# The fourth step of a sum of four, moved from GpSimd's additions to accumulating DMAs

## The chip, the cores and the metric

The kernel runs on one core of a Trainium2 chip. The metric is the device time of one execution in microseconds (us), given as the median of three runs. One further execution was profiled. Its engines are TensorE (PE in the rows; PEld are its weight loads), VectorE (DVE), ScalarE (ACT), GpSimd (POOL) and SyncE (SP, which here only issues DMAs).

## The reference

One decoder layer on x of shape (2, 2048, 512) in float32: self-attention, cross-attention and a mixture of experts, each followed by a residual sum and a layer norm. The change is in the self-attention:

```python
qkv = (x @ qkv_w + qkv_b).reshape(b, n, 3, H, D)     # H = 16, D = 32
q, k, v = jnp.moveaxis(qkv, 2, 0)
attn = jnp.einsum('bnhd,bmhd->bhnm', q, k) * scale
attn = jax.nn.softmax(attn, axis=-1)
out = jnp.einsum('bhnm,bmhd->bnhd', attn, v).reshape(b, n, c)
out = out @ proj_w + proj_b
```

The softmax's denominator is the sum over the keys of the exponentials. How that sum is formed is what is changed.

## The kernel before, in words

Self-attention takes units of four heads of one batch row (8 units), and in each unit chunks of 512 queries (4), so there are 32 chunks; the last one, `LAST`, is run apart. A chunk has 16 steps (`kt`), one for each tile of 128 keys.

In a step and for each of four heads `j`, TensorE does a maximum pass (`max_pass`, line 677, tile `sa_mx`: scores of the *next* chunk, of which VectorE takes the maximum over the keys, line 554) and a score pass (`score`, line 745, tile `sa_sc`: this chunk's scores, keys on the partitions, with the maximum already subtracted). ScalarE takes the exponential of each score bank (line 509) into `prob[:, kt % 4, j, :]`, a ring of four steps of 128x512 for each of four heads. There are three banks for maxima and two for scores, so TensorE runs at most that far ahead of VectorE and ScalarE. Every second step TensorE has a burst (`burst`): the products with the values for the two steps before (`add_values`, line 693, tile `sa_pv`), and, in steps with `kt % 4 == 2`, the row sums (`row_sums`, line 701, tile `sa_den`). Pieces of the projections of later units stand between the passes (lines 661 and 667, tile `sa_misc`); VectorE splits each finished projection in two parts (lines 546 and 548, tile `sa_hilo`), and SP moves these within SBUF to the operand stacks (line 279). SP also loads 1 MB blocks of the transposed input (line 348, tile `sa_xT`).

TensorE need not sum every step: four steps of exponentials are added elementwise first, into `quad_sum[:, d % 2]` (128 x 4 heads x 512, two buffers; `d` counts the sums, four in a chunk). The sum is made in halves of two heads (128x1024):

- `add_step(g, i, k)` on GpSimd, for k = 1, 2, 3, line 309: step k is added to the sum so far; for k = 1 the sum so far is step 0 itself. In front of it stands a wait for the exponentials of those heads, and for k > 1 a wait for the addition before.
- The second half of the first addition (k = 1, half 1) is VectorE's: `add_pair`, line 560, placed by `PAIR_AT = (2, 1)` in VectorE's order, after the second maximum of the third step of four.
- So there are five additions of GpSimd and one of VectorE for a sum (`ADDS = 5`), each announced by a semaphore: `quad_ready` for GpSimd's, `pair_ready` for VectorE's. `added(engine, d, k, half)` is the wait for one of them.

Who waits for a sum: TensorE's `row_sums(d)` for the last addition, half 1 of k = 3. It comes two steps after the sum's last step (`DEN_LAG = 6`). ScalarE, in `exponentials`, waits before it overwrites a ring place for the addition that read it: j = 0 and j = 2 of step `kt` wait for addition `max(kt % 4, 1)` of the sum before. The first addition of a sum waits for the row sums of the sum two before (`den_mm`), which read the same buffer.

The order on each engine is fixed by the program. GpSimd has the three `add_step` of each sum in turn, and once a chunk, after (i, k) = `DIVIDE_AT` = (1, 1), the division of the chunk before (line 315). VectorE has, in each step, four maxima, and at listed places the splits (`LEAVE_AT`), the pair's addition, the reciprocals (`INVERT_AT`, line 587) and the shift.

Of the kernel before, what the change touches and what calls it, by code (L numbers as in the profile page):

```python
# [9 lines left out]
ALU = mybir.AluOpType  # L10
# [57 lines left out]
def make_ident(pool, ident, zeroed, ready):  # L68

    pool.memset(ident[:, :], 0.0).then_inc(zeroed, 1)  # L70
    pool.wait_ge(zeroed, 1)
    pool.affine_select(out=ident[:, :], in_=ident[:, :], compare_op=ALU.not_equal, fill=1.0,
                       base=0, pattern=[[-1, P]], channel_multiplier=1).then_inc(ready, 1)


def self_attention(nc, z, keep, block, x, xT_dram, qkv_w, qkv_b, attnT_dram, rows_dram):


    B, N, C, KC, G, HG, D, T, NQ = z.B, z.N, z.C, z.KC, z.G, z.HG, z.D, z.T, z.NQ
# [15 lines left out]
    W, SKIP, SLOT_TILES, EMPTIES = C + 2, 2 ** 20, z.E * z.CAP // P, 2  # L95


    QUADS, ADDS = T // 4, 5
    PAIR_AT = (2, 1)
    DEN_LAG = 6  # L100


    LAST, LAST_DEN_AT = CHUNKS - 1, 11
# [60 lines left out]
    s = Stage(nc, left, "sa", keep)  # L164
# [9 lines left out]
    prob = s.sb("prob", [P, 4, HG, BANK])  # L174
    quad_sum = s.sb("quad_sum", [P, 2, HG, BANK])
# [38 lines left out]
    shift_mm, shiftT_ready, shift_in = s.sem("shift_mm"), s.sem("shiftT_ready"), s.sem("shift_in")  # L214
    sc_mm, prob_ready = s.sem("sc_mm"), s.sem("prob_ready")
    pv_mm, sums_ready, dens_ready, attn_ready = s.sem("pv_mm"), s.sem("sums_ready"), s.sem("dens_ready"), s.sem("attn_ready")
    pair_ready, quad_ready, den_mm, recip_ready = s.sem("pair_ready"), s.sem("quad_ready"), s.sem("den_mm"), s.sem("recip_ready")
    attn_out = [s.sem(f"attn_out{i}") for i in range(2)]
    made, emptied = s.sem("made"), s.sem("emptied")

# [5 lines left out]
    def after(engine, sem, value):  # L226

        if value > 0:
            engine.wait_ge(sem, value)

    def by_vector(d, k, half):
        return d < LAST * QUADS and (k, half) == (1, 1)

    def added(engine, d, k, half):

        if by_vector(d, k, half):
            engine.wait_ge(pair_ready, d + 1)
        else:
            at = 2 * (k - 1) + half
            engine.wait_ge(quad_ready, d * ADDS + at + (1 if d >= LAST * QUADS or at == 0 else 0))  # L240

    def max_turn(n):

# [25 lines left out]
    def move_stack(engine, i, heads, moved):  # L269

        job = JOBS[i]
        order = SPLITS.index(i)
        engine.wait_ge(hilo_ready, order + 1)
        for j in heads:
            for r, part in enumerate((0, 0, 1) if job.what == "q" else (0, 1, 0)):
                cols = slice(job.n * BANK, (job.n + 1) * BANK)
                rows = slice(D * r, D * (r + 1))
                dst = q_stack[rows, j, cols] if job.what == "q" else k_stack[job.unit % 2][rows, j, cols]
                engine.dma_start(dst.bitcast(F32), hilo[D * j:D * (j + 1), order % 2, part, :].bitcast(F32)).then_inc(moved[job.what, job.n], 16)
# [3 lines left out]
    @block.gpsimd  # L283
    def _(pool):
        make_ident(pool, ident, ident0, ident_ready)
        pool.wait_ge(ident_ready, 1)
        pool.memset(empty[:, :], 0.0).then_inc(made, 1)
        pool.wait_ge(made, 1)
        pool.memset(empty[:, C + 1:W].bitcast(I32), SKIP).then_inc(made, 1)
        for i in SPLITS:  # L290
            if JOBS[i].place is None:
                move_stack(pool, i, (2, 3), stacked_too)

        def add_step(g, i, k):


            d = g * QUADS + i
            if k == 1:

                after(pool, den_mm, d - 1)  # L300
            for half in range(2):
                if by_vector(d, k, half):
                    continue
                heads = slice(2 * half, 2 * half + 2)
                pool.wait_ge(prob_ready, (g * T + 4 * i + k) * HG + 2 * half + 2)
                if k > 1:
                    added(pool, d, k - 1, half)
                so_far = prob[:, 0, heads, :] if k == 1 else quad_sum[:, i % 2, heads, :]
                pool.tensor_tensor(quad_sum[:, i % 2, heads, :], so_far, prob[:, k, heads, :], ALU.add).then_inc(quad_ready, 1)  # L309

        def divide(g):

            pool.wait_ge(sums_ready, g + 1)
            pool.wait_ge(recip_ready, TQ * (g + 1))
            pool.tensor_tensor(recip[:, g % 2, :], sums[:, :], recip[:, g % 2, :], ALU.mult).then_inc(attn_ready, 1)


        for i in (2, 3):
            pool.wait_ge(out_x[i], 2 * 16)
        for g in range(LAST):  # L320
            for i in range(QUADS):
                for k in range(1, 4):
                    add_step(g, i, k)
                    if (i, k) == DIVIDE_AT and g > 0:
                        divide(g - 1)
        def last_adds():
            for k in range(1, 4):
                add_step(LAST, 0, k)
            divide(LAST - 1)

        tail.last_adds, tail.last_divide = last_adds, lambda: divide(LAST)
# [189 lines left out]
    def _(dve):  # L521
# [29 lines left out]
        def reduce_max(n, m):  # L551
            dve.wait_ge(max_mm, n + 1)
            q, j, k = m // (HG * KQ), m // KQ % HG, m % KQ
            dve.reduce_max(part_max[:, q, j, k:k + 1], max_bank(max_turn(n))[:, :], AX_X).then_inc(max_read, 1)  # L554

        def add_pair(d):

            after(dve, den_mm, d - 1)
            dve.wait_ge(prob_ready, (4 * d + 2) * HG)
            dve.tensor_tensor(quad_sum[:, d % 2, 2:4, :], prob[:, 0, 2:4, :], prob[:, 1, 2:4, :], ALU.add).then_inc(pair_ready, 1)  # L560

        def make_shift(g):

            dve.wait_ge(max_read, (g + 1) * NMAX)
            dve.reduce_max(top[:, :, :], part_max[:, :, :, :], AX_X).then_inc(top_ready, 1)

            after(dve, shift_mm, g)
            dve.wait_ge(top_ready, g + 1)
            dve.tensor_scalar(shift[:, :, :, 0], top[:, :, :], -1.0, None, ALU.mult).then_inc(shift_hi, 1)
            dve.wait_ge(shift_hi, g + 1)  # L570
            dve.scalar_tensor_tensor(out=shift[:, :, :, 1], in0=top[:, :, :], scalar=-1.0,
                                     in1=shift[:, :, :, 0].bitcast(F32), op0=ALU.mult, op1=ALU.subtract).then_inc(shift_ready, 1)

        def leave_shift(g):
            dve.wait_ge(shift_mm, g + 1)

            after(dve, shift_in, g * 16 * HG)
            dve.tensor_copy(shiftT[:, :], max_bank(shift_turn(g))[0:2 * HG, :]).then_inc(shiftT_ready, 1)

        def invert(g, q):  # L580

            if q == 0:
                dve.wait_ge(dens_ready, g + 1)

                after(dve, attn_out[g % 2], g // 2 * 16)
            cols = slice(q * P, (q + 1) * P)
            dve.reciprocal(recip[:, g % 2, cols], dens[:, cols]).then_inc(recip_ready, 1)
# [16 lines left out]
        for g in range(LAST):  # L604
            for kt in range(T):
                for i in range(PER_STEP):
                    n = (g + 1) * NMAX + LEAD + kt * PER_STEP + i
                    if n < CHUNKS * NMAX:
                        reduce_max(n, n % NMAX)
                    if i == SHIFT_AT and kt == T - EARLY and g + 1 < CHUNKS:  # L610
                        leave_shift(g + 1)
                    if (g, kt, i) in LEAVE_AT:
                        leave_psum(LEAVE_AT[g, kt, i])
                    if (kt % 4, i) == PAIR_AT:
                        add_pair(g * QUADS + kt // 4)
                    if (kt, i) in INVERT_AT and g > 0:
                        invert(g - 1, INVERT_AT.index((kt, i)))
                if kt == T - EARLY - 1 and g + 1 < CHUNKS:
                    make_shift(g + 1)
# [7 lines left out]
    def _(pe):  # L627
# [69 lines left out]
        def row_sums(d):  # L697

            added(pe, d, 3, 1)
            for j in range(HG):  # L700
                last = pe.matmul(den[D * j:D * (j + 1), :], ones[:, :], quad_sum[:, d % 2, j, :],
                                 start=(d % QUADS == 0 and d < LAST * QUADS), stop=(d % QUADS == QUADS - 1))
            last.then_inc(den_mm, 1)
# [1543 lines left out]
```

## Time and profile before

| | |
|---|---|
| median of three runs | 3635.53 us (3633.18 to 3640.7) |
| the profiled execution's own time | 3639.89 us |
| its span, first to last instruction | 3638.1 us |
| busy over the span | TensorE 93%, VectorE 74%, GpSimd 49%, ScalarE 46% |
| self-attention's chunks | from about 120 us to about 2130 us |

A line of a group says: line of the kernel, engine, operation, written tile and read tiles by the program's names, shapes (partitions x elements) and count, then busy time, mean of one in ns, and the idle time just before them with what ended it. In a timeline each row has the start, the duration (of all xN together) and in brackets the engine's idle time before and its releaser. A row of a stretch has its bounds and length, the busy us (and instructions) of TensorE, its weight loads, VectorE, ScalarE and GpSimd, then TensorE's granted clock, the DMA engines' busy share and GB/s. Busy time of TensorE is that of pipelined matmuls with modelled ends.

### The profile page before, as it was taken

How to read it: one execution, taken by the hardware profiler on the slowest of the kernel's cores; microseconds unless marked ns; L12 is line 12 of the kernel's file. 1: busy time of each engine (PE TensorE's matmuls, PEld its weight loads, DVE VectorE, ACT ScalarE, POOL GpSimd, SP SyncE). 2: the span in 40 equal slices, each digit the busy share in tenths (PEclk: the TensorE clock that was granted, in tenths of full speed). 3: DMA queues.
4: the chain of work that ended last, by engine and by line, in shares of the span. 5: the costliest groups of instructions: out<-in, count | busy, mean ns of one | idle time of the engine just before them, and what ended most of it. 6: DMA issues, size and time to landing. Idle time of an engine off the chain costs nothing. (4 is left out here: it accounts for less than half of the span.)

```text
span 3638.1 us, 51252 instructions
## 1 busy us (share of the span) xinstructions
PE 3389.5 (93%) x18533; PEld 2367.5 (65%) x18533; DVE 2691.6 (74%) x4636; ACT 1678.7 (46%) x3043; POOL 1795.2 (49%) x884
## 2 busy tenths in 40 slices
PE   7999999999999999999999987999959899999996
PEld 6555555555555555555555435877749788898885
DVE  5888788888888888888887845889734765566667
ACT  2455555555555555555555553444312332233332
POOL 2577777778777777777877840011110101110112
PEclk9999999999999999999999998999969999999998
DMA  6321222321322312312221022132132333323332
GB/s 219 105 58 49 89 70 64 94 59 60 102 59 66 92 51 83 87 59 77 74 61 31 15 94 66 58 121 93 48 125 70 114 120 108 107 96 106 128 119 98
DMA packets 190282, 308.54 MB, mean 85 GB/s; under 512 B 25514, under 2 KB 72234, under 8 KB 190011
## 3 DMA queue, kind: packets, MB, share of 16 engines
q1 hardware_dynamic: 166970, 243.82, 21.8%
q0 software_dynamic: 14592, 44.32, 3.5%
q10 hardware_dynamic: 8448, 16.78, 1.3%
q8 instruction: 171, 2.80, 0.3%
q14 instruction: 101, 0.82, 0.1%
HBM read 195.66 MB, written 61.33 MB: 71 GB/s over the span
## 5 line engine op out<-in xcount | busy, mean ns | idle before, releaser
L554 DVE TENSOR_REDUCE sa_part_max<-sa_mx 128x1 f32<-128x512 f32 x2048 | 1305.6, 681 | 357.6 <-PE sa_mx L677 326.7
L509 ACT ACTIVATE sa_prob<-sa_sc 128x512 f32<-128x512 f32 x2010 | 1107.3, 595 | 787.7 <-PE sa_sc L745 755.0
L309 POOL TENSOR_TENSOR sa_quad_sum<-sa_quad_sum,sa_prob 128x1024 f32<-128x1024 f32 x500 | 1258.6, 2537 | 210.4 <-ACT sa_prob L509 209.7
L2112 PE MATMUL ex_h<-ex_xT,ex_w 128*128 128x384 f32 (+2 forms) x2688 | 465.9, 329 | 53.4 <-issue 25.3
L677 PE MATMUL sa_mx<-sa_k_even,sa_q_stack 96*128 96x512 f32 x1024 | 483.3, 476 | 18.8 <-DVE sa_part_max L554 7.6
L2112 PEld LDWEIGHTS ex_h<-ex_xT,ex_w 128*128 128x128 f32 x2688 | 447.2, 195 | 65.7 <-issue 33.2
L677 PE MATMUL sa_mx<-sa_k_odd,sa_q_stack 96*128 96x512 f32 x1024 | 475.0, 464 | 13.8 <-DVE sa_part_max L554 9.4
L309 POOL TENSOR_TENSOR sa_quad_sum<-sa_prob 128x1024 f32<-128x1024 f32 x126 | 299.1, 2374 | 252.4 <-ACT sa_prob L509 252.4
L2123 PE MATMUL ex_acc<-ex_w,ex_hT 128*128 128x512 f32 x1719 | 416.2, 393 | 1.4 <-DVE ex_hT L2051 1.1
L745 PE MATMUL sa_sc<-sa_q_stack,sa_k_even 98*128 98x512 f32 x1024 | 412.2, 403 | 0.0
L745 PE MATMUL sa_sc<-sa_q_stack,sa_k_odd 98*128 98x512 f32 x986 | 402.5, 410 | 1.5 <-ACT sa_prob L509 1.5
L2123 PEld LDWEIGHTS ex_acc<-ex_w,ex_hT 128*128 128x128 f32 x1719 | 318.0, 189 | 64.9 <-issue 3.6
L1956 ACT ACTIVATE ex_h<-ex_h,ex_b 128x384 f32<-128x384 f32 x256 | 145.2, 580 | 385.6 <-PE ex_h L2112 385.6
L677 PEld LDWEIGHTS sa_mx<-sa_k_odd,sa_q_stack 96*128 96x128 f32 x1024 | 195.1, 191 | 172.2 <-issue 83.0
L677 PEld LDWEIGHTS sa_mx<-sa_k_even,sa_q_stack 96*128 96x128 f32 x1024 | 196.1, 192 | 170.1 <-issue 78.2
L1885 POOL DMA_DIRECT2D ex_xg<-rows x48 | 26.4, 554 | 531.4 <-PE ex_h L2091 531.1
L693 PE MATMUL sa_pv<-sa_prob,sa_v_odd 128*32 128x512 f32 x2048 | 252.8, 610 | 1.0 <-ACT sa_prob L509 1.0
L693 PE MATMUL sa_pv<-sa_prob,sa_v_even 128*32 128x512 f32 x2048 | 246.5, 599 | 0.0
L745 PEld LDWEIGHTS sa_sc<-sa_q_stack,sa_k_odd 98*128 98x128 f32 x986 | 188.4, 191 | 77.7 <-ACT sa_prob L509 54.7
L745 PEld LDWEIGHTS sa_sc<-sa_q_stack,sa_k_even 98*128 98x128 f32 x1024 | 195.8, 191 | 47.5 <-ACT sa_prob L509 22.9
L2049 DVE CAST ex_hT<-ex_h 128x384 fp32r<-128x384 f32 x256 | 94.4, 369 | 148.5 <-ACT ex_h L1956 147.8
L1138 POOL TENSOR_TENSOR ca_rstd<-ca_var_eps,ca_minus_half 128x8 f32<-128x8 f32 x16 | 26.5, 1654 | 324.1 <-DVE ca_var_eps L1206 324.1
(230 smaller groups left out, 4112.7 us busy)
## 6 DMA issues: line engine op xcount, KB each, us to landing
ex_w_in<-in_L_ffn_w_dram SPq DMA_DIRECT2D x130, 512.0 KB, 4.5
sa_xT<-xT SPq DMA_DIRECT2D x57, 1024.0 KB, 5.1
sa_q_stack<-sa_hilo SPq DMA_DIRECT2D x372, 64.0 KB, 2.0
rows<-sa_empty SPq DMA_DIRECT2D x48, 257.0 KB, 3.8
ex_rows<-rows POOLq DMA_DIRECT2D x8, 1542.0 KB, 8.4
sa_k_odd<-sa_hilo SPq DMA_DIRECT2D x192, 64.0 KB, 2.0
ex_xg<-rows POOLq DMA_DIRECT2D x48, 256.0 KB, 3.0
sa_k_even<-sa_hilo SPq DMA_DIRECT2D x168, 64.0 KB, 2.0
```

The source lines that it names most:

```text
L309: pool.tensor_tensor(quad_sum[:, i % 2, heads, :], so_far, prob[:, k, heads, :], ALU.add).then_inc(quad_ready, 1)
L509: act.activation(prob[:, kt % 4, j, :], score_bank(n)[:, :], ACT.Exp, scale=SCALE).then_inc(prob_ready, 1)
L554: dve.reduce_max(part_max[:, q, j, k:k + 1], max_bank(max_turn(n))[:, :], AX_X).then_inc(max_read, 1)
L677: pe.matmul(max_bank(max_turn(n))[:, :], q_stack[0:QK, j, at:at + P], k_stack[g // NQ % 2][0:QK, j, k * BANK:(k + 1) * BANK], start=True, ...
L693: last = pe.matmul(pv[D * j:D * (j + 1), :], v[buf][:, kt, D * j:D * (j + 1)], prob[:, kt % 4, j, :], start=(kt == 0), stop=(kt == T - 1))
L745: pe.matmul(score_bank(n)[:, :], k_stack[g // NQ % 2][0:AUG, j, kt * P:(kt + 1) * P], q_stack[0:AUG, j, g % NQ * BANK:(g % NQ + 1) * BANK] ...
L1138: pool.tensor_tensor(rstd[:, which, :, :], var_eps[:, which, :, :], minus_half[:, :, :], ALU.pow).then_inc(rstd_ready, 1)
L1885: pool.dma_start(xg[:, t, :], a.rows[row:row + P, 0:C]).then_inc(gathered, 16)
L1956: act.activation(h[:, j % 2, half * HALF:(half + 1) * HALF], h_bank[half][:, 0:HALF], ACT.Gelu, bias=b1[:, step:step + 1]).then_inc(h_read ...
L2049: dve.tensor_copy(hT[:, j % 2, 0, cols], h[:, j % 2, cols]).then_inc(hT_hi, 1)
L2112: last = pe.matmul(h_bank[half][:, 0:slots], w1[:, i % 2, pw, k, :], xT[:, e % 2, px, k, half * HALF:half * HALF + slots], start=(part == ...
L2123: last = pe.matmul(acc[t][:, :], hT[:, i % 2, ph, t * P:(t + 1) * P], w2[:, i % 2, pw, :], start=(i == 0 and part == 0), stop=(i == STEPS ...
```

## The change

The fourth step (k = 3) of every sum outside the last chunk is no longer added by an engine. GpSimd issues, for each half of two heads, a DMA from `prob` to `quad_sum` with `accum_op=ALU.add`: 128 rows of 4 KB, 512 KB in all, added into the target in SBUF. Both DMAs of a sum raise `quad_in` by 16, and the waits for the fourth step (TensorE's row sums, ScalarE's ring place) ask for 32 more with each sum. GpSimd issues each half after a wait for its exponentials and for its addition of k = 2. VectorE's `add_pair` and its semaphore are gone, and GpSimd makes that addition too: four additions of GpSimd for a sum (`ADDS = 4`) and two DMA issues. The last chunk's first sum keeps GpSimd's additions.

```diff
--- before.py
+++ after.py
@@ -95,8 +95,7 @@
     W, SKIP, SLOT_TILES, EMPTIES = C + 2, 2 ** 20, z.E * z.CAP // P, 2
 
 
-    QUADS, ADDS = T // 4, 5
-    PAIR_AT = (2, 1)
+    QUADS, ADDS = T // 4, 4
     DEN_LAG = 6
 
 
@@ -214,7 +213,7 @@
     shift_mm, shiftT_ready, shift_in = s.sem("shift_mm"), s.sem("shiftT_ready"), s.sem("shift_in")
     sc_mm, prob_ready = s.sem("sc_mm"), s.sem("prob_ready")
     pv_mm, sums_ready, dens_ready, attn_ready = s.sem("pv_mm"), s.sem("sums_ready"), s.sem("dens_ready"), s.sem("attn_ready")
-    pair_ready, quad_ready, den_mm, recip_ready = s.sem("pair_ready"), s.sem("quad_ready"), s.sem("den_mm"), s.sem("recip_ready")
+    quad_ready, quad_in, den_mm, recip_ready = s.sem("quad_ready"), s.sem("quad_in"), s.sem("den_mm"), s.sem("recip_ready")
     attn_out = [s.sem(f"attn_out{i}") for i in range(2)]
     made, emptied = s.sem("made"), s.sem("emptied")
 
@@ -228,16 +227,15 @@
         if value > 0:
             engine.wait_ge(sem, value)
 
-    def by_vector(d, k, half):
-        return d < LAST * QUADS and (k, half) == (1, 1)
+    def by_dma(d, k):
+        return d < LAST * QUADS and k == 3
 
     def added(engine, d, k, half):
 
-        if by_vector(d, k, half):
-            engine.wait_ge(pair_ready, d + 1)
+        if by_dma(d, k):
+            engine.wait_ge(quad_in, 32 * (d + 1))
         else:
-            at = 2 * (k - 1) + half
-            engine.wait_ge(quad_ready, d * ADDS + at + (1 if d >= LAST * QUADS or at == 0 else 0))
+            engine.wait_ge(quad_ready, d * ADDS + 2 * (k - 1) + half + 1)
 
     def max_turn(n):
 
@@ -299,12 +297,13 @@
 
                 after(pool, den_mm, d - 1)
             for half in range(2):
-                if by_vector(d, k, half):
-                    continue
                 heads = slice(2 * half, 2 * half + 2)
                 pool.wait_ge(prob_ready, (g * T + 4 * i + k) * HG + 2 * half + 2)
                 if k > 1:
                     added(pool, d, k - 1, half)
+                if by_dma(d, k):
+                    pool.dma_start(quad_sum[:, i % 2, heads, :], prob[:, k, heads, :], accum_op=ALU.add).then_inc(quad_in, 16)
+                    continue
                 so_far = prob[:, 0, heads, :] if k == 1 else quad_sum[:, i % 2, heads, :]
                 pool.tensor_tensor(quad_sum[:, i % 2, heads, :], so_far, prob[:, k, heads, :], ALU.add).then_inc(quad_ready, 1)
 
@@ -553,12 +552,6 @@
             q, j, k = m // (HG * KQ), m // KQ % HG, m % KQ
             dve.reduce_max(part_max[:, q, j, k:k + 1], max_bank(max_turn(n))[:, :], AX_X).then_inc(max_read, 1)
 
-        def add_pair(d):
-
-            after(dve, den_mm, d - 1)
-            dve.wait_ge(prob_ready, (4 * d + 2) * HG)
-            dve.tensor_tensor(quad_sum[:, d % 2, 2:4, :], prob[:, 0, 2:4, :], prob[:, 1, 2:4, :], ALU.add).then_inc(pair_ready, 1)
-
         def make_shift(g):
 
             dve.wait_ge(max_read, (g + 1) * NMAX)
@@ -611,8 +604,6 @@
                         leave_shift(g + 1)
                     if (g, kt, i) in LEAVE_AT:
                         leave_psum(LEAVE_AT[g, kt, i])
-                    if (kt % 4, i) == PAIR_AT:
-                        add_pair(g * QUADS + kt // 4)
                     if (kt, i) in INVERT_AT and g > 0:
                         invert(g - 1, INVERT_AT.index((kt, i)))
                 if kt == T - EARLY - 1 and g + 1 < CHUNKS:
```

## Rows read from the trace of the kernel before

**Rows 1.** Stretch from 300 to 2000, with the columns named above:

```profile
300.00:2000.00 1700.00, 1651.19 (x9293) 979.52 (x9286) 1400.81 (x2117) 954.41 (x1729) 1335.33 (x551) 0.99 0.24 70
```

**Rows 2.** Waits from 300 to 2000: us in total, times, longest us:

```profile
PEld sa_mx L677 <- DVE sa_part_max L554: 84.3, 155, 1.7
...
PEld sa_sc L745 <- ACT sa_prob L509: 45.3, 130, 0.4
...
PE sa_mx L677 <- DVE sa_part_max L554: 13.1, 51, 1.3
```

**Rows 3.** Groups of the additions, and durations by line (ns, min/median/max):

```profile
L560 DVE TENSOR_TENSOR sa_quad_sum<-sa_prob 128x1024 f32<-128x1024 f32 x124 | 180.3, 1454 | 0.3 <-ACT sa_prob L509 0.3
...
L560 DVE TENSOR_TENSOR sa_quad_sum<-sa_prob x124: 1214/1217/2348, 120.1 to 2106.6; 128x1024 f32<-128x1024 f32 x124
...
L309 POOL TENSOR_TENSOR sa_quad_sum<-sa_quad_sum,sa_prob x500: 2357/2380/3370, 120.3 to 2132.3; 128x1024 f32<-128x1024 f32 x167
```

**Rows 4.** Timeline around 611: an addition of VectorE behind a split:

```profile
610.33 0.75 DVE L548 SCALAR_TENSOR_TENSOR sa_hilo<-sa_misc,sa_qkb,sa_hilo 128x512 fp32r<-128x512 f32 x1
...
611.00 2.19 DVE L560 TENSOR_TENSOR sa_quad_sum<-sa_prob 128x1024 f32<-128x1024 f32 x1
...
611.98 0.40 PE L745 MATMUL sa_sc<-sa_q_stack,sa_k_odd 98*128 98x512 f32 x1
...
612.22 0.40 PE L677 MATMUL sa_mx<-sa_k_even,sa_q_stack 96*128 96x512 f32 x1
...
613.07 0.50 PE L745 MATMUL sa_sc<-sa_q_stack,sa_k_odd 98*128 98x512 f32 x1
...
613.85 0.50 PE L677 MATMUL sa_mx<-sa_k_even,sa_q_stack 96*128 96x512 f32 x1 [0.28 <-DVE sa_part_max L554]
...
614.62 0.60 ACT L509 ACTIVATE sa_prob<-sa_sc 128x512 f32<-128x512 f32 x1 [0.42 <-PE sa_sc L745]
```

**Rows 5.** Timeline from 1012 to 1033: one sum, engine by engine:

```profile
1012.82 2.36 POOL L309 TENSOR_TENSOR sa_quad_sum<-sa_prob 128x1024 f32<-128x1024 f32 x1 [2.35 <-ACT sa_prob L509]
1016.57 3.15 POOL L309 TENSOR_TENSOR sa_quad_sum<-sa_quad_sum,sa_prob 128x1024 f32<-128x1024 f32 x1 [1.39 <-ACT sa_prob L509]
1020.44 7.05 POOL L309 TENSOR_TENSOR sa_quad_sum<-sa_quad_sum,sa_prob 128x1024 f32<-128x1024 f32 x3 [0.72 <-ACT sa_prob L509]
1029.29 2.40 POOL L309 TENSOR_TENSOR sa_quad_sum<-sa_prob 128x1024 f32<-128x1024 f32 x1 [1.79 <-ACT sa_prob L509]
...
1016.27 1.21 DVE L560 TENSOR_TENSOR sa_quad_sum<-sa_prob 128x1024 f32<-128x1024 f32 x1
1019.04 4.07 DVE L554 TENSOR_REDUCE sa_part_max<-sa_mx 128x1 f32<-128x512 f32 x6 [1.56 <-PE sa_mx L677]
...
1022.05 2.27 ACT L509 ACTIVATE sa_prob<-sa_sc 128x512 f32<-128x512 f32 x4 [0.30 <-PE sa_sc L745]
...
1021.58 0.37 SPq L348 DMA_DIRECT2D sa_xT<-xT  x1
...
1032.89 1.04 PE L701 MATMUL sa_den<-sa_quad_sum,sa_ones 128*32 128x512 f32 x8
```

**Rows 6.** Groups: DMA issues on GpSimd:

```profile
L1907 POOL DMA_INDIRECT out_dram<-ex_out,ex_rows x48 | 67.3, 1401 | 71.2 <-DVE ex_out L2035 55.6 <-issue 8.6 <-DVE ex_out L2027 7.0
...
L1885 POOL DMA_DIRECT2D ex_xg<-rows x48 | 26.4, 554 | 531.4 <-PE ex_h L2091 531.1 <-POOL ex_minus_half L1879 0.3
...
L1890 POOL DMA_DIRECT2D ex_rows<-rows x8 | 7.2, 897 | 27.8 <-DMA out_dram<-ex_out,ex_rows 27.8
```

**Rows 7.** DMA issues: count, KB each, median us from issue to landing:

```profile
sa_xT<-xT SPq DMA_DIRECT2D x57, 1024.0 KB, 5.1
...
ex_rows<-rows POOLq DMA_DIRECT2D x8, 1542.0 KB, 8.4
...
sa_k_odd<-sa_hilo SPq DMA_DIRECT2D x192, 64.0 KB, 2.0
```

**Rows 8.** Stretch from 1024 to 1026, with the columns named above:

```profile
1024.00:1026.00 2.00, 2.00 (x18) 0.74 (x11) 0.91 (x2) 0.72 (x2) 2.00 (x2) 1.00 1.06 409
```

## The prediction

> **What bounds the kernel now.** I read the stretches first, because the change touches only self-attention. In the 1700 us from 300 to 2000, TensorE is busy for 1651.19 (97%) at a granted clock of 0.99, VectorE for 1400.81 (82%), GpSimd for 1335.33 (79%), ScalarE for 954.41 (56%) [rows 1]. TensorE sets the pace there. A VectorE or GpSimd instruction matters only where TensorE waits for it.
>
> The waits of the same stretch say how much that is. Weight loads of the maximum passes waited for VectorE 155 times, 84.3 us in all, but much of that lies under matmuls still running: the matmuls themselves stood idle for it for only 13.1 us. Score passes waited for ScalarE 130 times, 45.3 us [rows 2]. No row says that TensorE waits for the sum of four.
>
> Third, the groups: VectorE's one addition per sum (L560) runs 124 times, 31 chunks of four, mean 1454 ns, where the fastest and the median take 1214 and 1217. GpSimd's additions to the sum so far (L309) run 500 times, minimum 2357, median 2380, longest 3370 [rows 3]. A part of them is stretched where the two engines add side by side: in the timeline, 2.19 against 1.21 us on VectorE [rows 4, 5], 3.15 against 2.36 on GpSimd [rows 5].
>
> **What is removed.** L560, 180.3 us of VectorE. It mostly stands where VectorE has nothing to do: it is queued after the second maximum of the step in which TensorE sums values and rows, and that burst sends VectorE no maxima. The common case starts at 1016.27, takes 1.21, and VectorE then idles 1.56 us more until the next maximum [rows 5]. Cover: the burst; worth 0.
>
> The uncommon case is the gain. Where a projection leaves its bank in the same place, L548 runs ahead of L560, and L560 is also stretched: it starts at 611.00 and ends at 613.19, inside the next maxima. There the maximum pass follows the score of 613.07 only at 613.85, 0.78 us later, while an undisturbed pair has 612.22 - 611.98 = 0.24; TensorE loses 0.54. ScalarE, next in line, idles 0.42 before the exponential of 614.62 [rows 4]. So one such case gives back between 0.42, where ScalarE's exponentials take over as the late ones, and 0.54. I take 0.47. How many: with 1.217 and 2.19 us as the two kinds, the 180.3 us of 124 are (180.3 - 124 x 1.217) / (2.19 - 1.217) = 30, one for each of the 31 chunks [rows 3, 4]. Gain: 30 x 0.47 = **14 us**. Ends: 5 us, if most of it is handed to ScalarE's or other waits; 30 us, twice the 13.1 us of matmul idle scaled by 124 sums over the 105 in the stretch (13.1 x 124/105 = 15.5), for score passes that come earlier too.
>
> **What moves to GpSimd.** The second half of the first addition. GpSimd then has four additions of 2.38 a sum instead of five, and no neighbour that stretches them: 9.5 us instead of, in the sum at 1012.82, 2.36 + 3.15 + 7.05 = 12.6 [rows 3, 5]. Two DMA issues are added. GpSimd's plain issues take 554 ns (256 KB) and 897 ns (1542 KB) [rows 6]; an issue that adds is not in the trace. Below, 0.55; above, 1401 ns, an indirect one [rows 6]; I take 0.9, the largest plain transfer, since each row has an extra read. Sum 9.5 + 1.8 = 11.3 of the 16.5 us between 1012.82 and 1029.29 [rows 5]. It has room, so it costs 0. The divide, once a chunk, comes 2.4 us later; only SP's store five steps on waits for it. Nothing on SP or ScalarE moves; ScalarE's wait before it overwrites the fourth step asks for the landing, one whole sum later.
>
> **What is added on the path.** TensorE's row sums now wait for a landing. In the sum at 1012.82: the additions would run to 15.2, 17.6, 20.0, and the last from 1020.44, where its exponentials are ready as before, to 1022.8. The last two heads of the fourth step are ready at 1022.05 + 2.27/2 = 1023.2, the first two before 1022.05. So the first DMA is issued at 1022.8, the second near 1023.7. Before, the last addition ended at 1020.44 + 7.05 = 1027.5 and the row sums began at 1032.89 [rows 5]. The landing of the second DMA thus has 1032.89 - 1022.8 = **10.1 us from the first issue**. Each us beyond it falls on TensorE, 124 times over, for the maxima, scores and values of the next steps stand behind the row sums in its queue.
>
> How long the two take, 512 KB each, no row shows. Below: they land like one copy of 1024 KB, 5.1 us [rows 7]. Above: they read the target as well as the source, so 2048 KB, at the rate of the slowest large transfer GpSimd issues now, 1542 KB in 8.4 us: 11.2 us [rows 7]. Between: 2048 KB at the 409 GB/s that a stretch of full DMA engines shows [rows 8] is 5.1, and 2.0 for what a 64 KB move takes [rows 7]: 7.1. I take 7.1, since the neighbour by kind is the SBUF-to-SBUF move and by rate the full stretch. It leaves 3.0 us, and the wait costs 0. The cover is those 3 us.
>
> The row of a plain copy would by itself leave 5.0 us. The Trainium skill, in "Collectives: The Full Stack", section "The bandwidth ceiling: the fold count and why AG ≠ RS ≠ AR", says that a reducing transfer gets half the rate of a copying one because it reads two sources, and not because of the addition. By that rule the margin is 3.0 us instead of 5.0; no run here shows an adding DMA.
>
> **Sum.** The profiled execution took 3639.9 us around a span of 3638.1; 14 off gives 3625.9. The median of the runs is 3635.5, 4.4 lower, so I put the forecast at 3635.5 - 14 = **3621.5 us**.
>
> **Rivals.**
> *The landing is late in every sum (slower).* Place: the wait ahead of the row sums. It decides from 10.1 us after the first issue. At the upper end of 11.2 it costs 124 x 1.1 = 136 us, less the 14: 3758. If the two DMAs were served one after the other at the upper rate, far more. For it: the price of an addition inside a DMA is unseen, and each transfer is 128 rows of 4 KB twice. Against it: DMA share is only 0.24 in this stretch [rows 1]. Chance 0.28.
> *The landing is late in one sum of four only.* Once a chunk, an operand load of 1 MB is issued just before the additions, as at 1021.58 [rows 5]; it fills the DMA engines (1.06, 409 GB/s from 1024 to 1026 [rows 8]). If all of its 5.1 us [rows 7] stood ahead of the 7.1, the second landing would be near 1021.6 + 5.1 + 7.1 = 1033.8, 0.9 us late: 31 x 0.9 = 28, net 3621.5 + 28 = 3650; with half of it already moved, no loss. Chance 0.12, of which 0.04 ends within the noise and 0.08 slower.
> *The gain goes to ScalarE.* The 0.54 us of TensorE are taken over by its exponentials (45.3 us of waits of that kind now [rows 2]), of which only a third is then gained: about 5 us, 3630.5. Chance 0.13.
> *Forecast*, 3605 to 3630: 0.47.
>
> **How the numbers follow.** About 0.2%, 7 us, is what a measurement of this kernel can tell from no change. Faster: the forecast, 0.47. Same: 0.13 + 0.04 = 0.17. Slower: 0.28 + 0.08 = 0.36. The range begins at 3635.5 - 30 = 3605.5, say 3604, takes in the forecast, the ScalarE case and the single late sums (0.72), and of the late landings those up to 0.8 us late, 3621.5 + 124 x 0.8 = 3721 (0.08): 3604 to 3720. The forecast's own range is 3605 to 3630.
>
> **What would show it.** Right: no L560; GpSimd's additions all near 2.38; the wait of the maximum loads for VectorE down by some 15 us; adding DMAs landing about 7 us after the issue; row sums with no wait for a DMA. Wrong: a TensorE wait named after the DMA into the sum; its length times 124 is then the loss. If the landings are in time and the time is unchanged, score passes should wait longer for ScalarE. If GpSimd's issues take much more than 1.4 us, its last issue slips, and the margin with it.

## The result, and the profile after

Measured side by side, the changed kernel took **3739.48 us** (median of 4 runs, 3738.87 to 3740.58), the kernel before 3638.11 (4 runs): a ratio of 1.0273, 95% interval 1.0256 to 1.0289 (ratios and intervals are those on record; the quotient of two medians can differ a little, here 1.0279). It is slower by 101 us where 14 us less were forecast. In the profiled executions self-attention's chunks, from the first addition to the last product with the values, went from 2046.9 to 2149.2 us (+102.3); cross-attention (522.8 and 521.1) and the experts (950.7 and 949.9) stayed.

First the stretch from 300 to 2000, as in [rows 1]:

```profile
300.00:2000.00 1700.00, 1604.16 (x8840) 959.93 (x8840) 1201.52 (x1908) 903.54 (x1639) 1131.04 (x620) 0.96 0.56 130
```

VectorE and GpSimd do less, as foreseen. But TensorE is also busy for less (1604 instead of 1651), with fewer matmuls in the same time: it waits. For what, the waits of this stretch say, which answer to [rows 2]:

```profile
PEld sa_mx L668 <- DVE sa_part_max L553: 62.5, 112, 0.8
PEld sa_mx L668 <- DMA sa_q_stack<-sa_hilo: 62.2, 13, 5.2
PE sa_mx L668 <- DMA sa_q_stack<-sa_hilo: 59.7, 13, 5.0
...
PEld sa_sc L736 <- ACT sa_prob L508: 40.4, 123, 0.4
...
PE sa_mx L668 <- DVE sa_part_max L553: 4.2, 24, 0.2
...
PE sa_den L692 <- DMA sa_quad_sum<-sa_prob: 2.0, 5, 0.8
```

The wait for VectorE has shrunk from 13.1 to 4.2 us, and the row sums (`sa_den`) hardly wait for the new DMAs (2.0 us). What is new is a wait of 4.6 us, 13 times, of the maximum passes for a DMA that the change does not touch: SP's move of a split query block into `q_stack`. Over all of self-attention it is 64.3 us in 14 waits.

The groups and DMA issues of the page answer to [rows 3, 6, 7]:

```profile
L308 POOL TENSOR_TENSOR sa_quad_sum<-sa_prob 128x1024 f32<-128x1024 f32 x250 | 588.2, 2367 | 657.9 <-ACT sa_prob L508 657.8
L308 POOL TENSOR_TENSOR sa_quad_sum<-sa_quad_sum,sa_prob 128x1024 f32<-128x1024 f32 x252 | 596.1, 2376 | 68.0 <-ACT sa_prob L508 67.7
...
L305 POOL DMA_DIRECT2D sa_quad_sum<-sa_prob x248 | 215.9, 978 | 4.3 <-ACT sa_prob L508 3.9
...
sa_quad_sum<-sa_prob POOLq DMA_DIRECT2D x248, 512.0 KB, 6.5
```

The additions are no longer stretched, an issue takes GpSimd 0.98 us, and one adding DMA lands 6.5 us after it.

One of the 14 waits, from the timeline around 846:

```profile
837.43 8.51 SPq L277 DMA_DIRECT2D sa_q_stack<-sa_hilo  x12
...
842.69 1.75 POOL L305 DMA_DIRECT2D sa_quad_sum<-sa_prob  x2
...
846.37 0.61 PE L652 MATMUL sa_misc<-sa_wkv,sa_xT 128*128 128x128 f32 x4
851.34 0.79 PE L668 MATMUL sa_mx<-sa_k_odd,sa_q_stack 96*128 96x512 f32 x1 [4.36 <-DMA sa_q_stack<-sa_hilo]
```

In the third and fourth chunk of the first seven units the split block is one of the query blocks that the next unit's first maximum passes need (`k_odd`), at step 13 (`T - EARLY`). SP issues its 12 moves of 64 KB from step 10 on; GpSimd's adding DMAs now go out among the last of them. Their landings, first for this stretch, then for the same step before:

```profile
L277 SPq DMA_DIRECT2D sa_q_stack<-sa_hilo x12: 512/592/1617, 837.4 to 844.3; - x12
...
DMA to landing us min/median/max: 1.9/2.0/7.0
```

```profile
L279 SPq DMA_DIRECT2D sa_q_stack<-sa_hilo x12: 512/591/597, 805.8 to 812.7; - x12
...
DMA to landing us min/median/max: 1.9/2.0/2.0
```

The two adding DMAs among them:

```profile
L305 POOL DMA_DIRECT2D sa_quad_sum<-sa_prob x2: 854/996/1139, 842.7 to 843.3; - x2
...
DMA to landing us min/median/max: 5.1/6.5/8.0
```

Before, the last move was issued at 812.7 and landed 2.0 us later, at 814.7; this row shows when TensorE used it:

```profile
815.67 0.48 PE L677 MATMUL sa_mx<-sa_k_odd,sa_q_stack 96*128 96x512 f32 x1
```

The slack was 815.67 - 814.7 = 1.0 us. After, the last move, issued at 844.3, takes 7.0 instead of 2.0: 851.3, which is when the maximum pass starts. The second adding DMA lands at the same time (843.3 + 8.0). So it is in all 14 places: the last move lands within 0.5 us of the second adding DMA.

The wait is not the whole price. The stretches around it, with TensorE's granted clock as the third number from the end:

```profile
838.00:846.00 8.00, 8.00 (x47) 5.07 (x48) 5.19 (x9) 4.34 (x8) 6.43 (x5) 1.00 0.58 122
846.00:851.00 5.00, 0.98 (x7) 0.70 (x5) 1.73 (x5) 1.09 (x2) 0.00 (x0) 1.00 0.89 173
851.00:856.00 5.00, 4.66 (x15) 3.62 (x16) 2.08 (x3) 1.79 (x3) 1.80 (x1) 0.51 0.01 3
856.00:861.00 5.00, 5.00 (x34) 2.71 (x33) 2.57 (x4) 1.68 (x3) 4.01 (x3) 0.80 0.01 3
```

Behind this stand (a time in which TensorE stands idle) the clock is at its lower level of 1.2 GHz for five us and more (0.51), and a score pass takes 0.63 us instead of 0.40.

To put numbers on places, I took the time between the starts of neighbouring bursts of values (eight to a chunk) in each profiled execution, less the same interval before, and summed it by place, in us. The interval with the late query block is that from step 12 to 14, 14 times; VectorE's addition behind a split [rows 4] stands between steps 10 and 12, 28 times.

| kernel (as named below) | steps 12 to 14, 14x | steps 10 to 12, 28x | steps 2 to 8, 28x |
|---|---|---|---|
| after | +94.9 | -15.1 | +19.7 |
| e1_six | +2.5 | -15.0 | +18.7 |
| e2_two_of_16 | +2.4 | -15.1 | +14.2 |
| e4_copy | +41.6 | -15.1 | +14.8 |
| e5_hold | +1.3 | -15.0 | +3.2 |
| e6_late_moves | +53.2 | 0.0 | -0.2 |
| e9_later_moves | +94.6 | -0.1 | +3.7 |
| e7_third_pair | +1.5 | -15.1 | +18.6 |
| e8_half_waits | -0.3 | -15.0 | +13.6 |
| e11_inverts | +0.5 | -0.2 | -32.1 |
| e10_half_and_inverts | -0.3 | -15.1 | -28.7 |

So three things happened: the late moves cost 94.9 us, of which 64.3 are the waits and 30.6 the slow clock and the refilling of the engines behind them (2.2 each); the forecast gain is there, 15.1; and something between steps 2 and 8 gives it back (19.7). Together that is 99.5 of the 102.3 us.

### The profile page after: what moved, and what is told of

The parts are those of the page before. It is cut to its first block and busy times, and to the rows that moved or that the text cites. A ratio compares the mean times of both kernels' runs of the same rounds, so it can differ in the third digit from the quotient of the medians.

```text
span 3738.8 us, 51130 instructions
## 1 busy us (share of the span) xinstructions
PE 3430.5 (92%) x18533; PEld 2390.3 (64%) x18533; DVE 2522.9 (67%) x4512; ACT 1678.0 (45%) x3043; POOL 1627.7 (44%) x1008
## 3 DMA queue, kind: packets, MB, share of 16 engines
q0 software_dynamic: 50304, 174.36, 22.2%
## 5 line engine op out<-in xcount | busy, mean ns | idle before, releaser
L308 POOL TENSOR_TENSOR sa_quad_sum<-sa_prob 128x1024 f32<-128x1024 f32 x250 | 588.2, 2367 | 657.9 <-ACT sa_prob L508 657.8
L308 POOL TENSOR_TENSOR sa_quad_sum<-sa_quad_sum,sa_prob 128x1024 f32<-128x1024 f32 x252 | 596.1, 2376 | 68.0 <-ACT sa_prob L508 67.7
L668 PE MATMUL sa_mx<-sa_k_even,sa_q_stack 96*128 96x512 f32 x1024 | 491.9, 484 | 42.0 <-DMA sa_q_stack<-sa_hilo 30.4
L736 PE MATMUL sa_sc<-sa_q_stack,sa_k_even 98*128 98x512 f32 x1024 | 421.2, 411 | 0.0
L305 POOL DMA_DIRECT2D sa_quad_sum<-sa_prob x248 | 215.9, 978 | 4.3 <-ACT sa_prob L508 3.9
```

What stands on the lines that cost most here:

```text
L305: pool.dma_start(quad_sum[:, i % 2, heads, :], prob[:, k, heads, :], accum_op=ALU.add).then_inc(quad_in, 16)
L668: pe.matmul(max_bank(max_turn(n))[:, :], q_stack[0:QK, j, at:at + P], k_stack[g // NQ % 2][0:QK, j, k * BANK:(k + 1) * BANK], start=True, ...
L736: pe.matmul(score_bank(n)[:, :], k_stack[g // NQ % 2][0:AUG, j, kt * P:(kt + 1) * P], q_stack[0:AUG, j, g % NQ * BANK:(g % NQ + 1) * BANK] ...
```

## The experiments

**e1_six: GpSimd makes all six additions, no DMA adds.**

```diff
-    QUADS, ADDS = T // 4, 4
+    QUADS, ADDS = T // 4, 6
     def by_dma(d, k):
-        return d < LAST * QUADS and k == 3
+        return False
```

> No DMA takes part in the sums: GpSimd makes all six additions, VectorE none. Theory (the DMAs cost all of the loss, and VectorE's part of the change is a gain): the time falls under the kernel before by the 14 us of the prediction, 3624 us, with no TensorE wait for a DMA and the row sums as early as before. Rival (six additions of 2.37 and the division are 15.5 us in a period of 15.1 to 16.5, so GpSimd becomes the bound): row sums wait for GpSimd, up to 1 us in each of 124 sums, 3640 to 3750 us.

Measured: 3664.14 us, before 3642.0, ratio 1.0074 (1.0048 to 1.0100). That is what the rival foresaw (3640 to 3750), not the 3624 of the theory. Of the waits for a move only 5 are left in self-attention, 2.1 us in all, so it is the DMAs that bring them. GpSimd has room for a sixth addition in the first seven units; in the last, which has no projections and shorter steps, it has not (+17.1 us there).

**e2_two_of_16: the DMAs stay, but for the two sums of each unit that run beside the late moves**; there GpSimd adds all.

```diff
-        return d < LAST * QUADS and k == 3
+        return d < LAST * QUADS and k == 3 and d % 16 not in (10, 14)
...
```

> Of every sixteen sums, two (the third of the third and of the fourth chunk of a unit) get GpSimd's additions in place of the DMAs; the other fourteen keep the DMAs. Theory (the loss is made where the adding DMAs meet the moves to the query stack, in just these two): the 15 waits of the maximum passes for the moved queries, 68 us, and the slow clock behind them are gone, and the time is within 15 us of the kernel before, 3625 to 3640 us. Rival (the DMAs cost a little in every sum): only two sixteenths of the loss come back, 13 us of 101, about 3726 us.

Measured: 3645.6 us (10 runs), ratio 1.0013 (0.9998 to 1.0029): 5.6 us above the range of the theory, and far from the 3726 of the rival. Two of 16 sums carry the loss: 218 adding DMAs remain, and TensorE's waits for the moves are down to 2.0 us.

**e4_copy: the same DMAs, without the addition**; the row sums then leave out three steps of four.

```diff
-pool.dma_start(quad_sum[:, i % 2, heads, :], prob[:, k, heads, :], accum_op=ALU.add).then_inc(quad_in, 16)
+pool.dma_start(quad_sum[:, i % 2, heads, :], prob[:, k, heads, :]).then_inc(quad_in, 16)
```

> The two DMAs of a sum copy the fourth step over the sum instead of adding it, so the row sums leave out three of four steps; issues, bytes written and waits are the same. Theory (the engines are occupied by reading both source and target, and the moves stand behind that): the DMAs land in about 4.5 us in place of 6.6, the 15 waits of the maximum passes shrink from 4.5 to about 2 us or less and the time lies between, 3650 to 3700 us. Rival (only the number and size of the packets in the queue counts, not the adding): landings and waits stay, 3739 us.

Measured: 3694.11 us, ratio 1.0157 (1.0121 to 1.0192). Its landings and the share of the 16 DMA engines that GpSimd's queue took, then the waits:

```profile
q0 software_dynamic: 50304, 174.19, 12.6%
...
sa_quad_sum<-sa_prob POOLq DMA_DIRECT2D x248, 512.0 KB, 4.2
```

```profile
PE sa_mx L668 <- DMA sa_q_stack<-sa_hilo: 28.1, 14, 3.0
```

The moves are late behind copies too, by less: 28.1 us instead of 64.3. The last move again lands with the second of the two, 0.2 to 0.6 us behind it in all 14 places; only that one is there earlier. So the wait goes with the time that this traffic takes; that the addition by itself, beyond this time, adds nothing is not shown.

**e5_hold: in those two sums GpSimd waits for the query block to land before it issues.**

```diff
+                    late = LEAVE_AT.get((g, 10, 1)) if i == 2 and half == 0 and g % NQ >= 2 else None
+                    if late is not None:
+                        pool.wait_ge(stacked[JOBS[late].what, JOBS[late].n], stacked_by(late))
                     pool.dma_start(...)
```

> All DMAs as in the change, but in the two sums of sixteen where moves to the query stack are under way GpSimd issues them only after those moves have landed. Theory (order alone decides: the moves land in 2 us when nothing is ahead of them): no wait of the maximum passes for the moves, the adding DMAs start some 4 us later and land about at the row sums, which wait 0 to 2 us there; 3625 to 3650 us. Rival (DMA traffic as such slows the moves or TensorE): the loss stays above 3690 us.

Measured: 3664.04 us (3647.78 to 3675.23), ratio 1.0073 (1.0043 to 1.0102), above the 3650 that I had expected at most. The rows are from the fastest of its five executions (3647.78 us, granted clock 0.969; the others had 0.961 to 0.966), and so is its line in the table. The order of the two turns the wait around:

```profile
PE sa_den L695 <- DMA sa_quad_sum<-sa_prob: 18.1, 15, 2.1
...
PE sa_mx L671 <- DMA sa_q_stack<-sa_hilo: 0.8, 2, 0.5
```

The moves are in time; now the row sums wait, 18.1 us. With both in one place, one is late. Why the other four executions took 13 to 27 us more, no trace shows.

**e6_late_moves and e9_later_moves: the kernel before, no DMA in the sums, the late block's moves held back** until ScalarE's first (e6) or third (e9) exponential of step 11.

```diff
                 if job.what != "v":
+                    if job.what == "q" and g % NQ >= 2:
+                        sp.wait_ge(prob_ready, (g * T + 11) * HG + 1)
                     move_stack(sp, i, range(HG), stacked)
```

(e9: `+ 3` instead of `+ 1`.)

> The kernel before, with no DMA in the sums; SP only begins the moves to the query stack about 5.4 us later (after the first exponential of the twelfth step) in the third and fourth chunk of each unit. Theory (late moves alone, and the slow clock after the stall, are the whole price of the change): the maximum passes wait some 4.5 us at 14 or 15 places, the granted clock falls to about half behind each, and the time is the kernel before plus 14 x (4.5 + 2.4) = 97 us, about 3739 us. Rival 1 (the clock is not part of it): plus 64 us, 3706 us. Rival 2 (it was the traffic of the adding DMAs and not the lateness): less than 30 us over the kernel before.

> The kernel before, with all its additions as they were and no DMA in the sums; only the 12 moves of the late query block are held until ScalarE has made the third exponential of step 11, two more than in the run held to the first. One ScalarE exponential comes about every 1.03 us, so the moves should land some 2.1 us later and TensorE's 14 waits grow from 2.4 us each to about 4.5 us, near the 4.6 of the changed kernel: about 63 us in the wait list. If a late query block with the low granted clock behind the stall is the whole price of the change (theory), each stall costs about 2 us more than its wait, 14 x 2.0 = 28: the kernel takes before + 85 to 100 us, 3725 to 3740, a ratio of 1.023 to 1.027, about that of the changed kernel (1.0273), with no adding DMA in it. If instead the traffic itself also slows those steps (rival), only the wait and the refill seen in the shorter stall (1.4 each) return: 63 + 20 = 83 at the most, and less if the clock does not fall as far, 3705 to 3722.

Measured: e6 3696.61 us, ratio 1.0142 (1.0121 to 1.0164); e9 3732.18 us, 1.0251 (1.0233 to 1.0268). The waits, first e6, then e9:

```profile
PE sa_mx L679 <- DMA sa_q_stack<-sa_hilo: 33.2, 14, 3.3
```

```profile
PE sa_mx L679 <- DMA sa_q_stack<-sa_hilo: 63.7, 14, 6.0
```

In e6 the moves were late by less than I had expected (2.4 us each). With e9's 63.7 us of waits, the 14 intervals grow by 94.6, almost exactly what they do after the change (64.3 and 94.9), without one adding DMA. Late moves and what follows on them are the whole price in these intervals; the traffic costs nothing beyond. In e9 too the clock falls behind the stand:

```profile
839.50:843.40 3.90, 0.00 (x0) 0.00 (x0) 0.35 (x3) 0.00 (x0) 0.00 (x0) 0.91 0.42 97
843.40:849.00 5.60, 5.55 (x18) 4.35 (x19) 2.53 (x4) 1.82 (x4) 2.35 (x1) 0.50 0.01 3
```

**e7_third_pair: the kernel before, where GpSimd makes VectorE's addition in the third sum of each chunk alone** (that of [rows 4]), in the first seven units.

```diff
-        return d < LAST * QUADS and (k, half) == (1, 1)
+        return d < LAST * QUADS and (k, half) == (1, 1) and (d % QUADS != 2 or d >= 112)
...
```

> The kernel before, with no DMA in the sums; only in the third sum of each chunk of the first seven units GpSimd makes VectorE's addition too, the one that stands behind a split of a projection. Theory (the gain of the change is 0.5 us in each of these 28 sums, and GpSimd has room there): 14 us less than the kernel before, 3628 us. Rival (the gained time is given back, as in the run with six additions of GpSimd, where the granted clock was low more often): no difference from the kernel before, 3642 us.

Measured: 3642.76 us (12 runs), ratio 1.0006 (0.9995 to 1.0016). The 15.1 us are gained, and 18.6 lost between steps 2 and 8, with no DMA in it.

**e8_half_waits: the changed kernel with all its DMAs; the moves of heads 2 and 3 of the late block raise a semaphore of their own**, for which TensorE waits two steps later, at step 15, before the maximum passes that read them.

```diff
-                if job.what != "v":
+                if in_halves(job):
+                    move_stack(sp, i, (0, 1), stacked)
+                    move_stack(sp, i, (2, 3), stacked_late)
+                elif job.what != "v":
...
+                if kt == T - 1 and g + 2 < CHUNKS and (g + 2) % NQ < 2:
+                    o = ("q", (g + 2) % NQ)
+                    pe.wait_ge(stacked_late[o], stacked_late_by(job_of((g + 2) // NQ, *o)))
```

> The change with all its DMAs; the moves of the last two heads of the two late query blocks raise a semaphore of their own, and TensorE waits for it two steps later, where it first reads those heads. Theory (TensorE loses only by waiting for the last two moves): the first six moves are landed before the adding DMAs start, the last six have 7 us more, no wait of the maximum passes remains, and the time is 3625 to 3645 us. Rival (the traffic costs elsewhere): above 3690 us.

Measured: 3637.08 us (12 runs) against 3640.27 (23), ratio 0.9994 (0.9982 to 1.0006). The moves still land late, here in the same step, but nobody waits for them:

```profile
L284 SPq DMA_DIRECT2D sa_q_stack<-sa_hilo x12: 513/591/1568, 808.1 to 815.0; - x12
...
DMA to landing us min/median/max: 1.9/2.0/7.0
```

The change costs nothing once that wait is elsewhere; and it gains nothing, for 13.6 of the 15 us go between steps 2 and 8. There TensorE stands before a projection piece, in all kernels; before, and in e8:

```profile
264.47 1.10 PE L667 MATMUL sa_misc<-sa_xT,sa_wq 128*128 128x256 f32 x4 [1.40 <-DVE sa_hilo L548]
```

```profile
263.61 2.05 PE L672 MATMUL sa_misc<-sa_xT,sa_wq 128*128 128x256 f32 x4 [1.40 <-DVE sa_hilo L561]
```

The stand is the same, the clock behind it is not (1.00 before, 0.50 in e8):

```profile
265.00:268.00 3.00, 3.00 (x23) 1.49 (x25) 2.68 (x4) 1.09 (x2) 1.58 (x2) 1.00 0.31 70
```

```profile
265.00:268.00 3.00, 3.00 (x10) 1.54 (x12) 1.38 (x2) 1.19 (x2) 2.29 (x2) 0.50 0.31 72
```

Self-attention has 8 stretches of low clock before (34 us together), 11 in e8 (51), 17 in e7 (68), 20 in e1 (99), 30 after (160). Each kernel up to here has 21 of these stands, all in the first seven units and all but one of 1.4 us; every low stretch of those units before (5), in e8 (9), in e7 (15) and in e1 (15) begins at the end of one of them, at most 0.6 us before and 1.0 us behind it. And of what e7 loses between steps 2 and 8, all but 0.1 us lies in the 15 of 28 chunks in which it or the kernel before has the low clock there. Nor is it the profiled execution alone: over the whole kernel the granted clock was 0.962 to 0.966 in the 12 executions of e7, 0.965 to 0.971 in the 23 of the kernel before. So it is the clock that gives the gain back. Why it falls more often once VectorE's addition is gone stays open.

**e10_half_and_inverts and e11_inverts: that stand made shorter**, in e8 and in the kernel before. VectorE's split, for which TensorE stands at step 5, was queued behind four reciprocals of 0.94 us.

```diff
-    SUMS_AT, DENS_AT, DIVIDE_AT, STORE_AT = 0, 2, (1, 1), 10
-    INVERT_AT = ((3, 1), (3, 3), (4, 1), (4, 3))
+    SUMS_AT, DENS_AT, DIVIDE_AT, STORE_AT = 0, 2, (1, 3), 10
+    INVERT_AT = ((3, 1), (4, 1), (6, 1), (8, 1))
```

> The changed kernel with its late query block waited for in halves, and with VectorE's four reciprocals of a chunk spread into steps in which it stands idle (steps 3, 4, 6 and 8 instead of 3, 3, 4, 4), the division moved behind the third addition of the second sum. In all kernels so far TensorE stands 1.40 us, 21 times, 29 us in all, at step 5 before a projection piece, because VectorE's split of the piece before is queued behind those reciprocals; and in the kernels without VectorE's addition the three bursts around that place are 14 to 20 us longer in sum, with a granted clock of 0.50 behind it, which gives back the 15 us that the removal of that addition brings. Theory: the standing at step 5 is what the clock falls on. Then without it (0.4 us or less left of each 1.40, so 20 us less) the 14 us come back too: before - 4 - 20 - 14, about 3602, a ratio of 0.988 to 0.992. Rival: the clock falls anyway, or at the next stand: only the 20 us or less, 3616 to 3620, 0.993 to 0.995. Second rival: the reciprocals only delay other splits or the division: 3636 or more.

> The kernel before with the reciprocals and the division moved in the same way and nothing else, so that what the move brings by itself is seen: 20 us less of TensorE's stand at step 5 by the theory, and of the slow clock there only what the kernel before has (4 of its 8 slow stretches of self-attention, 3 us or less each): 3608 to 3622, a ratio of 0.992 to 0.996. The kernel with the change and the halves, run beside it, should be lower than this one by the 15 us of the change's own gain if nothing gives it back: 0.4% between the two; if the gain is given back elsewhere, the two are the same within 0.2%.

Measured, beside the same kernel before (3638.4 us, 9 runs): e10 **3587.85 us**, ratio 0.9863 (0.9848 to 0.9878); e11 3608.2 us, 0.9917 (0.9904 to 0.9931). The stands at step 5 in self-attention, first e11, then e10:

```profile
PE sa_misc L667 <- DVE sa_hilo L548: 21.2, 21, 1.0
```

```profile
PE sa_misc L672 <- DVE sa_hilo L561: 21.3, 21, 1.0
```

They are only 0.4 us shorter each (29.0 us in 21 before), 8 us in all where I had expected 20. But the interval from step 4 to 6 is 0.8 us or more shorter in each of 28 chunks, and only 1 (e11) and 2 (e10) stretches of low clock are left in self-attention, 3 and 7 us, none of them behind such a stand; from these two the 32.1 us of e11 come. And now the change's gain stays: e10 is 20.35 us below e11. In the profiled executions 12.9 of the difference lie in self-attention: -15.0 between steps 10 and 12, +3.4 between 2 and 8, the rest small; 5.3 lie in cross-attention, which the two kernels have in common, and were not followed up. e10 beats both kernels of this case; the larger part of it, e11, has nothing to do with the change.

## Why the prediction was wrong

- *TensorE sets the pace, and others matter only where it waits.* Right; the loss is a wait of TensorE and what its clock does behind it.
- *The gain, 30 cases of 0.47 us, 14 us.* Right: 28 intervals of 0.54 on average, 15.1, in all eight kernels without that addition. The place of [rows 4], after the change:

```profile
630.79 0.75 DVE L547 SCALAR_TENSOR_TENSOR sa_hilo<-sa_misc,sa_qkb,sa_hilo 128x512 fp32r<-128x512 f32 x1
632.64 2.48 DVE L553 TENSOR_REDUCE sa_part_max<-sa_mx 128x1 f32<-128x512 f32 x4 [1.10 <-PE sa_mx L668]
```

  VectorE is done with the split in time and now waits for TensorE. "The gain goes to ScalarE" did not happen (score passes' waits for ScalarE went from 45.3 to 40.4). But the gain was given back in another place, by the granted clock between steps 2 and 8, which was no rival of mine.
- *GpSimd has room: 11.3 us a sum.* Right: 4 x 2.37 + 2 x 0.98 = 11.4.
- *The landing: 7.1 us from the first issue, of 10.1.* The wait was forecast rightly (3.7 us in all of self-attention, 6 waits), the size too low: in the rows above the second lands 8.0 us after its issue, 8.6 after the first, and over the 124 sums it is 8.5 in the median (7.1 to 11.0). My 7.1 was thus the least, and the cover of 10.1 is what made the wait small. In 6 sums the landing took more than 10.1, each issued about 1.2 us behind a load of 1 MB: that is the second rival, and it cost 2.0 us of waits in 5 sums where I had put 28. Neither rival of late landings decided.
- *"Nothing on SP or ScalarE moves."* **This step failed.** SP's instructions did not move, but what they issue did: 12 moves with a slack of 1.0 us share the DMA engines with 1 MB of adding traffic, and the last of them lands 5 us later. I weighed the new DMAs against their own landing and against the one large load that goes out beside them, and never against the small transfers of the same steps, whose 2.0 us stood in [rows 7]. And I priced a late landing by its wait alone, where the slow clock and the refilling behind a stand of 4.6 us add 2.2.

In time of the DMA engines, GpSimd's queue takes 22.2 - 3.5 = 18.7% adding and 12.6 - 3.5 = 9.1% copying, above the 3.5% of the kernel before: a factor of 2.05. In landing time it is 6.5 against 4.2 us. With the first agrees the Trainium skill's rule that I weighed ("Collectives: The Full Stack", section "The bandwidth ceiling: the fold count and why AG ≠ RS ≠ AR"): half the rate for a transfer that reduces.

## What to carry to other kernels

When a change adds DMAs, list every transfer in flight in the same steps, whatever its size and queue, and the time between its landing and its first use; one with about 1 us to spare, as here, is where a loss can be, and letting its reader ask for it in parts can remove it. Price a new stand of TensorE as its wait and the slow clock behind it (here 4.6 + 2.2 us). And a gain of half a microsecond in a chunk is only kept if no later stand gives it to the clock: shortening that stand (here by spreading four reciprocals) can be worth more than the gain.

## What the runs showed of the hardware

- A 64 KB move issued behind two adding DMAs of 512 KB landed after 7.0 us instead of 2.0, at 851.3, as the second of them did (843.3 + 8.0), and one SP issue among them took 1.62 us instead of 0.59. Behind copies (e4) the last move lands 0.2 to 0.6 us after the second copy. What holds the move until then wasn't tried. The Trainium skill ("DMA: Bandwidth & Descriptors", section "Queues, rings and completion order") says that a DMA engine takes turns between queues packet by packet; how much of an adding DMA goes into one such packet no row shows, so whether these landings agree with it stays open.
- The granted clock fell to 0.50 or 0.51 behind the stands of 4.2 us and more, in all 14 places after the change and in e9, and 2.2 us were lost beyond each wait; behind those of 2.4 us on average (e6) it fell in 12 of 14, and 1.4 us were lost. Behind the stand of 1.40 us it stayed at 1.00 in one kernel and fell to 0.50 in another, with the same work around it; behind the 21 of 1.0 us each in e10 and in e11 it never fell. The Trainium skill ("TensorE: Matmul & The Clock Gate", Part 1, section "What's actually happening") says that activity is watched over a window that runs free of the kernel, so that where in it a stand falls would matter; no run here shows that window, and what decides stays open.
